# ScalarE's edge loop begins at the first instruction slot of a fetch page, in both graph-attention layers

## What is computed

```python
def _gatv2(x, edge_index, Wl, bl, Wr, br, att, bias):
    loops = jnp.arange(n)
    src = jnp.concatenate([edge_index[0], loops])
    dst = jnp.concatenate([edge_index[1], loops])
    xl = (x @ Wl + bl).reshape(n, h, d)
    xr = (x @ Wr + br).reshape(n, h, d)
    e = jax.nn.leaky_relu(xl[src] + xr[dst], NEG_SLOPE)
    score = jnp.einsum('ehd,hd->eh', e, att)
    m = jax.ops.segment_max(score, dst, num_segments=n)
    ex = jnp.exp(score - m[dst])
    denom = jax.ops.segment_sum(ex, dst, num_segments=n)
    alpha = ex / denom[dst]
    out = jax.ops.segment_sum(alpha[:, :, None] * xl[src], dst, num_segments=n)
    return out.reshape(n, h * d) + bias
...
x_in = _gatv2(x, edge_index, Wl1, bl1, Wr1, br1, att1, bc1)
h = _batchnorm(x_in @ W1 + b1, g1, be1)
h = jax.nn.relu(h)
h2 = _gatv2(h, edge_index, Wl2, bl2, Wr2, br2, att2, bc2)
```

## Time and profile before

| | us |
|---|---|
| median of 3 runs | 6345.56 |
| lowest and highest of them | 6339.74, 6350.01 |
| the profiled execution | 6317.56 |
| its span, first to last instruction | 6315.4 |
| edge stage of layer 1, first score to end of the first turn | 153.50 |
| 26 turns of ACT's loop, layer 1 | 1426.00 |
| edge stage of layer 2, first score to end of the first turn | 152.90 |
| 26 turns of ACT's loop, layer 2 | 1583.50 |

### The profile page before, as it was taken

How to read it: one execution, slowest core, us unless ns; L and a number is a source line. 1 busy time by engine, 2 the same in 40 slices (tenths; PEclk the granted TensorE clock), 3 DMA queues, 4 the chain that set the end, 5 groups by cost and what they waited for, 6 DMA issues and landing times. The chain is left out here.

```text
span 6315.4 us, 122309 instructions
## 1 busy us (share of the span) xinstructions
PE 4846.5 (77%) x22358; PEld 2873.2 (45%) x22359; DVE 5297.8 (84%) x12463; ACT 4432.6 (70%) x19858; POOL 4274.3 (68%) x3722
## 2 busy tenths in 40 slices
PE   3799689558988888888788888888888766666563
PEld 2575345234444444444644444444444445555552
DVE  9998898659999999999678898988888766666666
ACT  6487679429999999999278888888888553333332
POOL 0488777837777777776576676666666557777773
PEclk9999999779999999999899999999999977777776
DMA  0243000235555555556154444544445234444444
GB/s 16 54 86 30 2 2 2 31 116 144 140 139 140 137 141 139 140 139 114 27 152 130 125 129 127 131 124 127 129 125 124 42 106 130 128 129 128 129 129 77
DMA packets 342152, 657.19 MB, mean 104 GB/s; under 512 B 99030, under 2 KB 190100, under 8 KB 341506
## 3 DMA queue, kind: packets, MB, share of 16 engines
q0 software_dynamic: 191520, 481.83, 30.7%
q1 hardware_dynamic: 150370, 172.99, 10.7%
HBM read 618.58 MB, written 34.84 MB: 103 GB/s over the span
## 5 line engine op out<-in xcount | busy, mean ns | idle before, releaser
L1332 POOL DMA_INDIRECT feat_area<-xl_table,gather_col x1856 | 2178.9, 1174 | 948.3 <-issue 531.1
L1382 PE MATMUL bank<-node_area,feat_area 128*128 x3712 | 1481.2, 523 | 331.9 <-DVE feat_area L1524 146.2
L1458 ACT ACTIVATE feat_area<-feat_area 128x128 f32<-128x128 f32 x5104 | 1608.6, 419 | 145.8 <-issue 145.8
L1474 ACT ACTIVATE feat_area<-feat_area 128x130 f32<-128x130 f32 x5568 | 1500.4, 331 | 256.2 <-DVE feat_area L1532 254.4
L1395 PE MATMUL bank<-feat_area 128*128 128x390 f32 x3712 | 1433.4, 509 | 138.6 <-ACT feat_area L1458 90.2
L1382 PEld LDWEIGHTS bank<-node_area,feat_area 128*128 128x128 f32 x3712 | 646.9, 193 | 954.1 <-issue 701.7
L1474 ACT ACTIVATION_READ_ACCUMULATOR feat_area<-feat_area 128x1 f32 x5568 | 1054.3, 190 | 0.0
L1395 PEld LDWEIGHTS bank<-feat_area 128*128 128x128 f32 x3712 | 694.6, 195 | 694.8 <-issue 293.8
L2020 POOL DMA_INDIRECT feat_area<-kv_table,gather_src x832 | 808.1, 971 | 280.6 <-issue 252.1
L1524 DVE TENSOR_TENSOR feat_area<-bank,feat_area 128x780 f32<-128x780 f32 x928 | 890.0, 959 | 62.4 <-DMA feat_area<-xl_table,gather_col 43.8
L650 POOL DMA_INDIRECT word_by_dst<-feat_area,gather_col x640 | 791.8, 1237 | 195.0 <-issue 188.9
(11 more groups left out here) (363 smaller groups left out, 7140.4 us busy)
## 6 DMA issues: line engine op xcount, KB each, us to landing
feat_area<-lo_slot SPq DMA_DIRECT2D x464, 128.0 KB, 3.3
feat_area<-xl_table,gather_col POOLq DMA_INDIRECT x1856, 3.5
feat_area<-lo_slot_src SPq DMA_DIRECT2D x104, 256.0 KB, 3.4
node_area<-lo_edge SPq DMA_DIRECT2D x100, 256.0 KB
xl_table<-feat_area SPq DMA_DIRECT2D x98, 195.0 KB, 2.2
feat_area<-kv_table,gather_src POOLq DMA_INDIRECT x832, 2.8
feat_area<-gates SPq DMA_DIRECT2D x348, 32.0 KB
feat_area<-rowgates SPq DMA_DIRECT2D x696, 0.1 KB
```

The source lines that it names most:

```text
L1332: pool.indirect_dma_start(ring[:, at:at + HE], None, k.xl, bass.IndirectOffsetOnAxis(ap=rows, axis=0)).then_inc(gathered[s], 16)
L1382: last = nc.tensor.matmul(pair[s % 2][:, u, 0:HE], pick[s // 2 % 2][:, c:c + P], k.node[:, ds(columns[0], HE)], start=True, stop=True)
L1458: last = nc.scalar.activation(row[:, 0:D], row[:, 0:D], ACT.Copy, scale=row[:, D:D + 1])
L1474: last = nc.scalar.activation(at, at, ACT.Copy, accum_out=score_in[s // CG][:, to:to + 1])
```

## The change

`pipeline` takes two new arguments, `head` and `hint`, and opens the loop with the module's `Fori` for its own engine alone. [...] With `head=None` and `hint=False` the loop is opened as it was. One caller passes `head=0`: ACT's pipeline in `gat_edges`, which both layers use. `hint` is left at False everywhere. No instruction of any loop body is added, removed or moved within the body.

```diff
-def pipeline(eng, groups, stages, unroll=2, number=False):
+def pipeline(eng, groups, stages, unroll=2, number=False, head=None, hint=False):
...
-    with eng.Fori(first, last) as i:
+    with eng.bass.Fori(first, last, engines=(eng.engine,), head_slot=None if head is None else {eng.engine: head},
+                       hint_back_edge=hint) as i:
         for s in range(unroll):
             at(i, s)
...
-            pipeline(act, groups, [(-3, exps), (-11, weight), (0, reduce)], U)
+            pipeline(act, groups, [(-3, exps), (-11, weight), (0, reduce)], U, head=0)
```

## The result

The changed kernel takes 6180.51 us (median of 4 runs, 6174.09 to 6183.77) against 6345.5 us before: a ratio of 0.9739, with a 95% interval of 0.9722 to 0.9756. The profiled execution took 6174.09 us, its span 6172.0 us.

A forecast was written before the change was run, and what follows sets the result against it. Layer 2's ACT loop, refetched every turn, was taken to stall PE and DVE. Saving 157.5 us less 2.8 us for entry, 154.7 us off 6345.56, gave 6190.9 us, range 6160 to 6230 us.

The forecast's parts named there:

- The cause: ACT's loop in layer 2 is fetched anew each turn, layer 1's is held; 157.5 us between the layers.
- Term (1): Layer 2: moving the head of ACT's loop to a fetch page's first slot saves 26 x 6.06 = 157.5 us.
- Term (2): Layer 1: the head of ACT's loop moves too, but the loop is held already, so 0 us.
- Term (3): Loop entries: a jump over the padding costs 2.8 us in layer 1, 0 in layer 2; bounds 0 and 19.4.
- Term (4): Other callers of the helper pass no head and no hint and open the loop as before: 0.
- A: Rival: the padding is lost between compiled and loaded stream, so nothing is gained, 6345.6 us; chance 0.05.
- B: Rival: one stall per branch stays in layer 2 and layer 1 gains one, 6332 us; chance 0.03.
- C: Rival: fetching ahead overwrites the loop's first page, layer 1 refetches every turn, 6505.9 us; chance 0.05.
- The chain: ACT's stall holds up PE's sums, then DVE at L1615; DVE is 97% busy, so it counts almost in full.
- The clock: PE's granted clock in layer 2's 26 turns rises from 0.95 to 1.00 once the pauses go.
- T: ACT's code: four blocks of 128 instructions held; entering one fetches the next, so 313 slots stay with head up to 71.

The follow-up runs named there:

- Experiments 1: Kernel before, unaligned, with 20 one-element ScalarE copies ahead of layer 1's edge stage, moving both loops 20 slots: 6221.13 us, ratio 0.9829.
- 10: Kernel before with two one-element ScalarE copies ahead of layer 2's loop, first run: 6172.5 us profiled; its plain execution, 6331.53 us at low clock, was left out.
- 5: Changed kernel with the head at slot 0 in layer 1 alone, layer 2 not aligned: 6169.46 us, ratio 0.9734.
- experiment 2: Changed kernel with layer 1's head at slot 71 and layer 2's at slot 72: 6287.99 us, ratio 0.9931.
- experiment 3: Changed kernel with layer 1's head at slot 100 and layer 2's at slot 228: 6287.1 us, ratio 0.9929.
- the second pair: Kernel before and changed kernel, both unchanged, profiled and run again: 6340.43 and 6171.17 us, ratio 0.974.
- experiment 11: Repeat of the kernel before with two one-element ScalarE copies ahead of layer 2's loop and nothing else: 6170.01 us, ratio 0.9728.

## Why the prediction was right

- *The cause.* That layer 2's loop was fetched anew on each turn, and that this was all that parted the layers, was read off two stretches of one trace. Experiments 1 and 10 show it without the edit, and 5 with the edit in the other layer alone: where the head lies by count decides, in either layer. The result by itself could not tell blocks of 128 from pages of 256, since slot 0 is good with both, as the prediction says. Experiments 1 to 3 settled that the four blocks of 128 it preferred are right. Its counted offsets, about 125 and 56, were one slot short: they are 126 and 57.
- *Term (1), 157.5 us.* The turns gave 157.0 us, and 157.9 in the second pair.
- *Term (2), 0 us in layer 1.* Its 26 turns took 1428.7 us against 1426.0; over all these kernels a held loop takes 1425.8 to 1431.3 us, so this is nothing.
- *Term (3), +2.8 us.* This was mis-sized: the jumps cost 0.44 and 0.42 us, 0.9 us together, as the target of both was loaded: no packet falls into either gap. No run shows an entry by a jump that costs nothing, as the term has it for layer 2; the least is 0.14 us, in layer 2 of experiment 2. From slot 57 of its block, layer 1's head moved by 71 slots or by 199 to come to slot 0; the short gap with no packet in it speaks for 71, into the next block. That the module's count runs over more than one block is seen in layer 1 of experiment 3: packets come 1.6 and 5.1 us behind the copy ahead of the loop, one for the entry into a new block by the jump and one for the entry 28 slots further on. A jump from slot 57 to slot 100 of one block would have given the second alone.
- *Term (4), 0.* ACT's loops behind the edge loop move with the padding as well. From the end of layer 2's last turn to the end it is 1356.4 us before and 1356.1 after, and in the last edge stage ACT waits 735.5 us for DVE, against 734.5.
- *The rivals.* A and B did not happen: 12 packets in both layers, 26 gaps of at most 0.3 us. C did not: layer 1 is as it was. Its idea, a fetch ahead that overwrites the loop's first block, is nevertheless the reading of what the kernel before suffers in layer 2. Experiment 2 shows where it decides, and slot 0 is 72 slots from it.
- *The size.* 6190.9 us was forecast, 6180.51 measured, inside the range of 6160 to 6230. Term (3) is 1.9 us of the 10.4. The medians moved by 165.0 us and, in the second pair, by 169.3 us, while the traces show 157 to 158 in the turns. The interval of the ratio (0.9722 to 0.9756) just holds 157.0 / 6345.5, a ratio of 0.9753. Whether plain executions of the kernel before lose a little more to its stalls than the profiled ones, or chance in the stages ahead of layer 1 (12 us between executions) makes the rest, stays open, and with it the other 8.5 us. The fast end of the range put the 28.0 us by which the plain runs are longer into the stalls. The second profiled execution of before took 18.6 us more than the first (6336.21), 12.7 of them ahead of layer 1's turns and only 2.5 in layer 2's.
- *The chain.* DVE's wait at L1615 went with ACT's gaps, and the stall had counted in full: 6.06 us a turn for gaps of 5.4. But the claim doesn't hold for smaller gaps. In experiment 3, ACT's gaps grew by 67 us in layer 1 (73.1 against 6.0) and the turns by 57.9 us. ACT waits 66.4 us for DVE in the 26 held turns, 2.6 us in each, and 57.8 us in experiment 3: 8.6 of the missing 9.2 us came out of that wait.
- *The clock* was 1.00 in both layers' turns, as expected. The prediction cites the earlier trace rows for its fall in layer 2; the digits there are 9 in both layers, and it is the earlier trace rows that shows it, 1.00 and 0.95.

Experiments 2 and 3 measured blocks of 128, four of them held by T's reading, and an edge between slots 71 and 72. A packet stands at each entry into a block (experiment 3), and the block fetched ahead is what T has as the cause of the loss: from slot 126 of a block a loop of 313 slots ends at 439 and would have fitted four blocks of 128 (512 slots), if not for that block.

## What to carry to other kernels

Where one loop appears twice, cut both at the same turns: a difference in idle time with no releaser, once or twice per branch back, together with packets on the instruction queue, is a loop whose code doesn't stay. Then the place of its first instruction is a parameter like any other, and an edit ahead of it can cost or give 2.6% or more (two copies in experiment 11: ratio 0.9728), so compare kernels only with the queue's packets beside their times. Align the head of such a loop, or hint its branch back; here either was enough (12 packets in each layer, ratios 0.9739 and 0.9756). Only this loop's length, 313 slots (314 with the hint), was run.

## What the runs showed of the hardware

- ACT's instructions came in packets of 8 KB, 128 slots: with the head at 100, three packets of a turn stand 0.4 to 1.4 us ahead of its records 29, 157 and 285 (experiment 3). The loop of 313 slots stayed where it ends within the third block (head at 71: 12 packets in 26 turns), and nothing of it did with its closing branch in the fourth (head at 72: 142, five more a turn).
- A refetching turn cost 2.1 to 2.3 us more than a held one with the head at 77, 100 or 228, 4.3 us at 72, 6.06 us at 126 and 6.7 us at 127. Between these runs it goes by how much work lies between the head and the next block: one gap of mostly 2.4 to 3.3 us with 28 slots or more (100 and 77), two gaps with two (52 at 126, 140.3 us), one double gap with one (26 at 127, 158.0 us). At 72 the gaps are 4.2 us each; that the useless fetch makes them so is argued from the times of its packets.
- With a hint for the branch back ACT's loop made no fetches: 12 packets in place of 142, with the head at 72 and at 100.
- A jump to a loaded block cost 0.42 to 0.44 us at eight entries and 0.14 us at one (layer 2 of experiment 2), where running on into the loop showed no gap. A branch back whose target had to be fetched cost 2.4 to 3.3 us in nearly all turns with the head at 126, 77, 100 or 228.
- Behind a pause of 5.61 us in PE its granted clock was 0.57 over 7 us, against 1.00 at the same place of layer 1; without the pauses the clock of the 26 turns went from 0.95 to 1.00.
